# Graph layer with a two-expert feed-forward on one core: four GpSimd operations per quad move to VectorE, and one low part is made inside the row statistics

## The reference, cut to what matters

```python
xf = layernorm(x)                                   # 12500 x 256
h = gelu(xf @ W1[e] + b1[e])                        # for the two chosen experts e: 12500 x 512 each
y = sum(gate[e] * (h[e] @ W2[e] + b2[e]))           # 12500 x 256
out = x + layer_norm(y + xf) * gamma + beta         # layer_norm over the 256 values of a row
```

## Time and profile before

| | |
|---|---|
| time, median of 3 runs | 3031.16 us (3028.17 to 3031.72) |
| the profiled execution | 3025.19 us, of which the span of its records is 3023.7 us |
| TensorE clock over the whole span | 0.835 of full speed (2.4 GHz) |
| stage 5 | from about 2411 us to the end |
| quads 2 to 23, 2462.23 to 2990.52 us | 528.29 us for 22 quads, TensorE clock 1.00 |

### The profile page before, as it was taken

One profiled execution on the slowest core, in us unless ns is written; L12 is line 12 of the kernel. 1 busy time (PEld: TensorE's weight loads), 2 busy tenths in 40 slices (PEclk: granted clock), 3 DMA queues, 4 the chain that ended last, 5 costly groups with the idle time before them and its releaser, 6 DMA issues.

```text
span 3023.7 us, 38535 instructions
## 1 busy us (share of the span) xinstructions
PE 2475.3 (82%) x11532; PEld 1605.7 (53%) x11532; DVE 1724.4 (57%) x3502; ACT 774.0 (26%) x1810; POOL 1991.1 (66%) x1831
## 2 busy tenths in 40 slices
PE   6888778787887788778877887788778699999997
PEld 5665434443444344434444444444444388888886
DVE  7885455445545554555455545554555566666666
ACT  4553011111111111111111111111111155555554
POOL 5446777777777777777777777777777334444443
PEclk9998777877787777777877787877777799999999
DMA  5333344434444444444444444444444322111221
GB/s 143 107 101 97 115 125 123 120 116 123 125 118 118 124 124 116 122 124 125 116 121 124 124 118 120 124 126 116 121 123 125 94 70 62 62 62 62 66 75 49
DMA packets 192238, 327.01 MB, mean 108 GB/s; under 512 B 32703, under 2 KB 138216, under 8 KB 192200
## 3 DMA queue, kind: packets, MB, share of 16 engines
q0 software_dynamic: 80160, 219.14, 25.4%
q1 hardware_dynamic: 111624, 107.01, 11.3%
q10 hardware_dynamic: 416, 0.39, 0.1%
HBM read 275.21 MB, written 51.20 MB: 108 GB/s over the span
## 4 chain that ended last, share of the span: by engine, by line
POOL 28%; PE 26%; issue 20%; DVE 15%; DMA 7%; ACT 2%; POOLq 0%; DVEq 0%; ACTq 0%; SPq 0%
POOL ring L643 20%; PE pd L1015 8%; PE pa L1076 6%; PE pd L1042 6%; DMA ring<-xn_table,idxb 4%; PE pc L1093 2%; POOL work L672 2%; POOL work L657 2%; POOL work L655 2%; DVE bst L1184 2%; PE pc L1003 2%; DMA work<-x_rows 2%; DVE nh L1211 1%; DMA out<-work 1%; DVE nv L1206 1%
## 5 line engine op out<-in xcount | busy, mean ns | idle before, releaser
L643 POOL DMA_INDIRECT ring<-xn_table,idxb x1661 | 1607.5, 968 | 509.7 <-issue 489.9
L1076 PE MATMUL pa<-ring,ohh 128*128 128x512 f16 x1661 | 767.7, 462 | 222.5 <-DMA ring<-xn_table,idxb 206.5
L1354 DVE TENSOR_REDUCE ring<-pa 128x256 f32<-128x512 f32 x196 | 135.4, 691 | 586.1 <-PE pa L1076 585.5
L1093 PEld LDWEIGHTS pc<-ohh,ones_h 128*1 128x1 f16 x2045 | 133.7, 80 | 535.7 <-issue 535.7
L1093 PE MATMUL pc<-ohh,ones_h 128*1 128x128 f16 (+1 forms) x2045 | 384.7, 219 | 0.0
L1076 PEld LDWEIGHTS pa<-ring,ohh 128*128 128x128 f16 x1661 | 173.1, 104 | 350.1 <-issue 172.1
L1136 PE MATMUL pd<-parts 128*128 128x256 f32 (+1 forms) x1568 | 314.6, 284 | 33.8 <-DVE parts L1524 33.8
L1136 PEld LDWEIGHTS pd<-parts 128*128 128x128 f32 (+1 forms) x1568 | 253.4, 188 | 51.4 <-DVE parts L1524 44.4
L1334 DVE TENSOR_TENSOR ohh<-iota_f,edges 128x512 f16<-128x512 f32 (+1 forms) x391 | 272.8, 718 | 0.9 <-issue 0.9
L997 PE MATMUL pd<-work,KS_s 128*128 128x256 f32 x196 | 100.7, 669 | 198.6 <-DVE work L1388 198.6
L769 ACT ACTIVATE work<-pd 128x512 f32<-128x512 f32 (+1 forms) x49 | 29.2, 596 | 881.5 <-PE pd L981 881.5
(11 more groups left out here) (188 smaller groups left out, 3684.0 us busy)
## 6 DMA issues: line engine op xcount, KB each, us to landing
ring<-xn_table,idxb POOLq DMA_INDIRECT x1661, 2.7
yT<-in_x SPq DMA_DIRECT2D x24, 512.0 KB, 4.0
xn_table<-ring SPq DMA_DIRECT2D x24, 512.0 KB, 4.8
work<-in_x SPq DMA_DIRECT2D x48, 256.0 KB
x_rows<-work SPq DMA_DIRECT2D x48, 256.0 KB
y_rows<-work SPq DMA_DIRECT2D x48, 256.0 KB
work<-y_rows SPq DMA_DIRECT2D x24, 512.0 KB, 4.3
work<-x_rows SPq DMA_DIRECT2D x24, 512.0 KB, 4.0
```

What stands on the lines that cost most here:

```text
L643: pool.indirect_dma_start(out=msgs[:, k, :, :].rearrange("p s d -> p (s d)"), out_offset=None, in_=xn_table[:, :], in_offset=bass.Indirect ...
L1076: ins = mm(pa[:, t % 2, :], oh[:, slot, :], msgs[:, k, :, :].rearrange("p s d -> p (s d)"), start=begins, stop=ends, skip_group_check=True)
L1093: ins = mm(pc[0:1, v, c0:c1], ones_h[:, 0:1], oh[:, slot, o0:o1], start=first, stop=closing, skip_group_check=True)
L1354: V.tensor_reduce(strips[:, (NS * u + t + 1) % KEPT, :], pa[:, t % 2, :].rearrange("p (s d) -> p d s", s=PARTS), AX.X, ALU.add)\
```

## The change

The four GpSimd operations are written in VectorE's program, with the same tiles and semaphores. GpSimd has nothing left in stage 5. `pre_add` (`y_in += b2m`) of quad q-1 now stands behind the low part of chunk 0 of quad q, `add_beta` behind that of chunk 5, `scale_z` behind chunk 6, `finish` behind chunk 7. From quad 1 on, the low part of chunk 3 is no longer made behind the row statistics but inside them, behind the second of their 12 square root steps. The data and the formulas are the same.

```diff
@@ gpsimd
-            def stage5(q, u):
...
-                pool.wait_ge(s[f"yin_loaded{u}"], 2 * quad_dmas(q, u))
...
-                pool.tensor_tensor(y_in[u][:, 0:n, :], y_in[u][:, 0:n, :],
-                                   b2m[:, :].unsqueeze(1).to_broadcast([P, n, D]), ALU.add).then_inc(s["yb_made"], 1)
-                pool.tensor_tensor(x1_in[u][:, 0:n, :], x1_in[u][:, 0:n, :],
-                                   beta_b[:, :].unsqueeze(1).to_broadcast([P, n, D]), ALU.add)\
-                    .then_inc(s["xb_made"], 1)
-                if not is_int(q, 0):
-                    finish(q - 1, 1 - u)
...
-            over_quads(pool, stage5)
-            finish(NQ, 0)
@@ vector
+            def pre_add(q, u):
+
+                dve.wait_ge(s[f"yin_loaded{u}"], 2 * quad_dmas(q, u))
+                dve.wait_ge(s["b2_made"], 1)
+                n = len(tiles_of(q))
+                V.tensor_tensor(y_in[u][:, 0:n, :], y_in[u][:, 0:n, :], bc(b2m[:, :], n), ALU.add)\
+                    .then_inc(s["yb_made"], 1)
+
+            def add_beta(q, u):
+
+                n = len(tiles_of(q))
+                V.tensor_tensor(x1_in[u][:, 0:n, :], x1_in[u][:, 0:n, :], bc(beta_b[:, :], n), ALU.add)\
+                    .then_inc(s["xb_made"], 1)
...
+            def scale_z(q, u):
+
+                n = len(tiles_of(q))
+                dve.wait_ge(s["zn_made"], q + 1)
+                V.tensor_tensor(z[u][:, 0:n, :], z[u][:, 0:n, :], bc(gamma_b[:, :], n), ALU.mult).then_inc(s["f_scaled"], 1)
+
+            def finish(q, u):
+
+                n = len(tiles_of(q))
+                dve.wait_ge(s["f_scaled"], q + 1)
+                dve.wait_ge(s["xb_made"], q + 1)
+                V.tensor_tensor(x1_in[u][:, 0:n, :], x1_in[u][:, 0:n, :], z[u][:, 0:n, :], ALU.add)\
+                    .then_inc(s["fin_made"], 1)
 
             def stage5(q, u):
+                later = not is_int(q, 0)
                 for f in range(NF):
-                    hidden(q, f)
+                    if not (later and f == 3):
+                        hidden(q, f)
...
+                    if f == 0 and later:
+                        pre_add(q - 1, 1 - u)
...
-                    if f == 2 and not is_int(q, 0):
-                        stats_z(q - 1, 1 - u)
+                    if f == 2 and later:
+                        stats_z(q - 1, 1 - u, [(2, lambda: hidden(q, 3))])
                     if f == 4 and not is_int(q, NQ):
                         split_y(q + 1, 1 - u)
+                    if f == 5 and later:
+                        add_beta(q - 1, 1 - u)
+                    if f == 6 and later:
+                        scale_z(q - 1, 1 - u)
+                    if f == 7 and later:
+                        finish(q - 1, 1 - u)
             over_quads(dve, stage5)
+            pre_add(NQ, 0)
+            add_beta(NQ, 0)
             add_y(NQ, 0)
             stats_z(NQ, 0)
+            scale_z(NQ, 0)
+            finish(NQ, 0)
```

More of the change, by code:

```diff
@@ L647, in _ @@
             over_blocks(pool, stage3)
-            def stage5(q, u):
-                tail = is_int(q, NQ)
-                n = len(TAILS) if tail else QT
-                pool.wait_ge(s[f"yin_loaded{u}"], 2 * quad_dmas(q, u))
-                if is_int(q, 0):
-                    pool.wait_ge(s["b2_made"], 1)
-                pool.tensor_tensor(y_in[u][:, 0:n, :], y_in[u][:, 0:n, :],
-                                   b2m[:, :].unsqueeze(1).to_broadcast([P, n, D]), ALU.add).then_inc(s["yb_made"], 1)
-                pool.tensor_tensor(x1_in[u][:, 0:n, :], x1_in[u][:, 0:n, :],
-                                   beta_b[:, :].unsqueeze(1).to_broadcast([P, n, D]), ALU.add)\
-                    .then_inc(s["xb_made"], 1)
-                if not is_int(q, 0):
-                    finish(q - 1, 1 - u)
[L663 to L673, removed]
-            over_quads(pool, stage5)
-            finish(NQ, 0)
         @block.scalar
@@ L1538, in add_y, with stats_z @@
                                     y_in[u][:, 2 * pr:2 * pr + 2, :], ALU.add).then_inc(s["z_made"], 1)
-            def stats_z(q, u):
+            def stats_z(q, u, fill=()):
                 tiles = tiles_of(q)
@@ L1544, in stats_z @@
                 row_stats([(z[u][0:n, t, :], n) for t, n in tiles], "f_bn", "f_mv", "f_rstd", "f_stats", q + 1,
-                          rstd2[:, 0:len(tiles)], nmr2[:, 0:len(tiles)])
+                          rstd2[:, 0:len(tiles)], nmr2[:, 0:len(tiles)], fill)
+            def scale_z(q, u):
[8 more added lines that the diff above has]
+                    .then_inc(s["fin_made"], 1)
             def stage5(q, u):
+                later = not is_int(q, 0)
                 for f in range(NF):
-                    hidden(q, f)
+                    if not (later and f == 3):
+                        hidden(q, f)
                     if is_int(q, 0) and f < 3:
                         (lambda: split_w1(1), lambda: split_w2(1), mix_b2)[f]()
-                    if f == 1 and not is_int(q, 0):
+                    if f == 0 and later:
+                        pre_add(q - 1, 1 - u)
+                    if f == 1 and later:
                         add_y(q - 1, 1 - u)
-                    if f == 2 and not is_int(q, 0):
-                        stats_z(q - 1, 1 - u)
+                    if f == 2 and later:
+                        stats_z(q - 1, 1 - u, [(2, lambda: hidden(q, 3))])
                     if f == 4 and not is_int(q, NQ):
                         split_y(q + 1, 1 - u)
+                    if f == 5 and later:
[4 more added lines that the diff above has]
+                        finish(q - 1, 1 - u)
             over_quads(dve, stage5)
+            pre_add(NQ, 0)
+            add_beta(NQ, 0)
             add_y(NQ, 0)
             stats_z(NQ, 0)
+            scale_z(NQ, 0)
+            finish(NQ, 0)
 _INS = ["x", "src", "dst", "L0_gnn_W_l", "L0_gnn_b_l", "L0_gnn_W_r", "L0_mix_wq", "L0_mix_bq", "L0_mix_wk", "L0_mix_bk",
```

## The result

| | before | after |
|---|---|---|
| time, median of 4 runs each | 3029.66 us (3027.2 to 3031.72) | 2990.12 us (2988.5 to 2995.36) |
| ratio | | 0.9873, 95% interval 0.9858 to 0.9888 |
| span of the profiled execution | 3023.7 us | 2989.4 us |
| start of quad 2 to start of tail (first Gelu each) | 528.29 us, 24.01 per quad | 495.51 us, 22.52 per quad |
| start of tail to the end of the last addition | 29.07 us | 24.09 us |

The account below looks back on a forecast made before the run. TensorE was taken as the bound, 95% busy in quads 2 to 23. Quads 30.6, tail 3.3 and last two operations 1.2 us give 35.1 us: 3031.16 - 35.1 = 2996.1 us, range 2987 to 3012.

Parts of the forecast that it names:

- The bound and the stall: Quads 2 to 23: TensorE bounds, waiting once per quad for a low part; removing it wins 22 x 1.39 = 30.6 us.
- each part alone removes it: Quads: moving GpSimd's work alone ends the stall; low part 3 inside the statistics comes 2.1 us earlier still.
- low part 2 by 2.1 us: Ahead of the statistics: GpSimd's b2m addition prolongs low part 2 to 2.81 from 0.69 us, delaying what follows some 2.1 us.
- The rule held against the forecast: Shared SBUF read port of VectorE and GpSimd: offloading between them might not help; time would stay near 3031 us.
- The allowance of a low part: Low part 3 in quad 1: may queue for 3.6 us before TensorE notices; at most 1.2 us of queueing expected.
- The price of the moved operations: Four operations on VectorE: 1.22 us each, taken from split_y, 4.9 us per quad, hidden behind TensorE.
- Rival 3: Slower: moved operations cost 2.70 us each on VectorE, which becomes the bound at 24.4 us per quad; 3040 us; chance 0.03.
- the forecast 17 to 18.5: VectorE in quads: busy 17 to 18.5 us per quad, upper figure from quad 1's 13.63 + 4.9.
- Rival 1: From low part 2 to split_y: moved work makes its own stall, 15.3 us stay, 3011 us; chance 0.10.
- Rival 2: No change: shared port, or the statistics alone and not GpSimd being the cause; 3031 us; chance 0.05.
- The tail: Tail: half of three TensorE waits totalling 6.6 us, so 3.3 us won; last two operations on VectorE win 1.2 us.
- 15 us of cover for the loads: pre_add's wait for the quad's loads: they are issued early enough to leave 15 us of cover.

Follow-up runs that it names:

- long_add_nofill: move_only plus one useless GpSimd addition of 128x1280 per quad, begun when z is made; another chip: 3865.16 us, ratio 0.9979, quads 23.72 us.
- move_only: Changed kernel with the low part of chunk 3 back behind the row statistics, the four operations still on VectorE: 2990.46 us, ratio 0.9877.
- fill_only: Kernel before with only the low part of chunk 3 moved inside the statistics, GpSimd keeping its four operations: 2997.22 us, ratio 0.9900.
- load_once_more: Changed kernel with one useless VectorE addition of 128x1024 behind each of the four moved operations: 2994.84 us, ratio 0.9888.
- load_twice_more: Changed kernel with two useless VectorE additions behind each of the four moved operations: 3081.39 us (one run), quads 25.56 us.
- second_pair_moved: Kernel before with only scale_z and finish moved to VectorE, low part 3 behind the statistics: 3028.50 us, ratio 1.0000.
- first_pair_moved: Kernel before with only pre_add and add_beta moved to VectorE, low part 3 behind the statistics: 2996.06 us, ratio 0.9893.
- long_add_fill: Changed kernel plus one useless GpSimd addition of 128x1280 per quad, begun when z is made; another chip: 3837.13 us, ratio 0.9906, quads 22.52 us.
- idle_adds_nofill: move_only plus two useless GpSimd additions of 128x1024 per quad, begun when z is made: 2993.55 us, ratio 0.9883, quads 22.67 us.
- idle_memsets_nofill: move_only plus two GpSimd memsets of 128x2048 per quad; another chip: 3805.97 us (one run, time not used), quads 22.52 us.
- tail_order: Changed kernel with only the operations at the end of VectorE's program reordered; another chip: 3839.44 us, ratio 0.9908, tail 23.20 us.

## Why the prediction was right

**The bound and the stall.** TensorE was the bound, its one wait per quad was what could be won, and it went. Forecast 30.6 us, measured 32.8. The term was the mean of 22 quads less quad 1. The mean holds one short quad, the last, as the tail's first Gelu comes early (23.29 us before, 21.82 after); the middle quads took 24.04 and take 22.56. Taking a full quad's 22.62 us off that mean gave 1.39 us in place of 1.49.

**The total.** The forecast was 35.1 us, the medians give 39.5: the quads gave 2.2 us more, the tail 0.5, and 1.6 came from a place that was not in the sum. The forecast of 2996.1 us lies 6.0 above the measured 2990.12, since it starts from a median of 3031.16 us for the kernel before, which is 3029.66 with one more run: 1.5 us on top. The causes in the sum were right; their sizes were all somewhat small, and one term was missing.

**Its cause.** Shown: additions on GpSimd that nobody needs bring the stall back in `long_add_nofill`, and the place of low part 3 takes it away again. The prediction said that each part alone removes it, which `move_only` and `fill_only` show. It was incomplete in who is held up. The "low part 2 by 2.1 us" holds for 13 of 22 quads; in the other 9 it is the second square root step, by 2.15. The length of the hold-up is what counts, as both stand ahead of low part 3. The rule held against the forecast, that work moved between engines that get in each other's way changes only who waits, did not come true: `move_only` won 36.5 us.

**The allowance of a low part**, worked out as 3.6 us from the start of the Gelu, is 3.4 by TensorE's own start (2453.49 in quad 1, the Gelu 2453.69); it was tested up to 2.4 and held. For low part 3 of the order before it is about one us behind unhindered statistics, as the prediction had it, and two doses agree: 1.05 us of hold-up cost 0.14 us per quad, 2.1 us cost 1.20 in `long_add_nofill` (23.72 - 22.52), so 0.9 us went unnoticed in both. The kernel before fits the same sum. From the start of low part 2 to the end of low part 3 it takes 8.10 us, `move_only` 5.74 (2608.14 to 2613.88). The 2.36 us more, less 0.9, give 1.46; its quads lost 1.49. Some 0.2 us of this is the first square root step (L1206), which GpSimd holds up in 21 of the 22 quads, 0.31 us and more for 0.17.

**The price of the moved operations** was 1.22 us, the row of the same engine and shape. Rival 3 (the price of GpSimd, 2.67 to 2.73) fell. Its sum was too dark as well: VectorE is busy for 16.0 us per quad, not the forecast 17 to 18.5, since the 13.63 us of quad 1 hold two low parts of 1.75 and 2.12 us that GpSimd prolonged. Without the moved work it needs 16.0 - 4.9 = 11.1 us, and with 2.70 us for each moved operation, an estimate from these figures, 21.9 of 22.52. `load_once_more`, 2.44 us in each place, has no stall; `load_twice_more`, 3.66 us, has one. Rival 1, a stall of its own, fell with `load_once_more`. Rival 2, no change, was the right forecast for one half of the change only: `second_pair_moved`.

**The tail.** Forecast 3.3 + 1.2 us, measured 5.0: L1537 of the last rows (`add_y`) starts 16.95 us after the tail's first Gelu in place of 20.83, 3.9 us; the last two operations take 1.42 us in place of 2.60, 1.2 us. So the half that I took of the three waits was slightly small: they went from 6.6 us to 1.8, and the two additions of the tail's own rows put some 1.2 us on the chain, where they start at 2978.55 and 2979.15, directly ahead of L1523. What moving adds to the fill lies here: `fill_only` and the changed kernel have the same quads, and tails of 28.46 and 24.09 us, and behind the tail's last addition another 1.5 us.

**Not forecast:** the 1.6 us between the last addition and the end of the span. They are no scatter. The three kernels whose last addition is GpSimd's (before, `fill_only`, `first_pair_moved`) need 4.1 us from there to the end; the eleven whose last addition is VectorE's need 2.5 to 2.6, also where GpSimd has other work in stage 5. The profile puts the difference down to a last wait of SP for TensorE's queue, 1.7 us against 0.2. So it comes with moving `finish`, and belonged in the sum; why the end takes longer behind GpSimd is open.

**Open.** The forecast's 15 us of cover for the loads was not tested by taking it away; the trace after has no wait of VectorE for a transfer in quads 2 to 23. The clock stayed at 1.00 in quads 2 to 23 although TensorE no longer pauses. That the fill brings anything beyond the move in the total is not shown: 2990.12 and 2990.46 us. It takes 0.9 us off the tail and gives the order 2.1 us of room, which `long_add_fill` needed and the changed kernel does not.

## What to carry to other kernels

Before judging an engine by its busy time, compare the same instruction with itself: a VectorE row of 0.69 us that sometimes takes 2.8 is held up, and the other engine's row that overlaps it names by whom. Then ask which instruction stands behind it and how much room that has; here hold-ups of 1.0 and 1.5 us at low parts 6 and 7 (`first_pair_moved`) were harmless, and one of 2.1 us ahead of low part 3 cost most of 1.5 us per quad. Where such a stall can be removed by moving work or by order alone, try the order first: it moved one low part and took the time down by 1.00%, the moved work alone by 1.23%, both together by 1.27%.

## What the runs showed of the hardware

- Which of the two engines is prolonged goes by who starts first: GpSimd's addition 0.13 us ahead, VectorE's takes 2.81; VectorE's 0.15 us ahead, GpSimd's takes 2.80 in place of 2.40 (`fill_only`). In the 22 quads of the kernel before it is so each time. The Trainium skill ("SBUF — State Buffer", section Who interferes with whom) describes a lock on a shared pair of ports, held for the whole instruction; these numbers agree.
- How long the second one is prolonged can be worked out: by what the first still has to run, less 0.14 us. The rows give it in five places: low part 2 of the earlier trace rows (2.26 us left, 2.81 = 0.69 + 2.26 - 0.14), low part 2 of `idle_adds_nofill` beside an addition of 1.89 us from 2650.07 (1.22 left, 1.77), low part 7 of `first_pair_moved` beside one of 2.74 us from 2668.10 (1.58 left, 2.13 for the 2.14 shown), the step of `fill_only` (2.30 left, 2.33 for 2.32) and that of `idle_memsets_nofill` (0.58 left, 0.61 for 0.60).
- The same section says that a VectorE instruction with two inputs in SBUF contends with a GpSimd instruction that reads SBUF and not with one that only writes. `idle_memsets_nofill` agrees: 0.69 us beside a memset.
- Not in the prediction: a `tensor_scalar` of four elements per row is held up as long as a large operation, 2.32 us for 0.17 beside an addition, and also beside a memset (0.60 us). The statistics (L1184, 1.40 us for four) kept their time beside GpSimd's additions: 87 of their 88 instructions in quads 2 to 23 of the kernel before overlap one, and all take 0.40 to 0.42 us.
- An addition of 128x1024 takes 1.22 us on VectorE and 2.39 us on GpSimd (`pre_add`) when nothing holds them up. Where both inputs are the same values, as in the useless ones, GpSimd takes 1.89 us (`idle_adds_nofill`) and VectorE still 1.22 (`load_once_more`).
- Two chips differed by 28% in the whole (3028 and 3878 us for the kernel before) and not at all in quads 2 to 23: 22.52 us on both. On the slower one GpSimd stood idle for 1343.4 us ahead of its gathers, in place of 509.7; its row, from `tail_order`:

```profile
L643 POOL DMA_INDIRECT ring<-xn_table,idxb x1661 | 1613.8, 972 | 1343.4 <-ACT idxb L704 649.5 <-issue 470.1 <-remote 202.2
```
